# A fused two-layer gated block on one core: 16 bit integer outputs in the quantized feed-forward, the last norm in two parts with writes by ScalarE, and four banks for output products

## What is computed

```
x = x + tanh(g_xattn[0]) * attention0(layernorm(x), ctx)
x = x + tanh(g_ffn[0])   * experts(layernorm(x))          # 8 experts, top 2 of the first 1024 tokens
x = x + tanh(g_xattn[1]) * attention1(layernorm(x), ctx)
x = x + tanh(g_ffn[1])   * quantized_ffn(layernorm(x))
```

```
act_qdq(x)  : s = max(|x| over all of x) / 32767;  clip(round(x / s), -32768, 32767) * s
x    = act_qdq(x)
up   = act_qdq(x @ lpbq_dequant(w_up).T)          # w in 4 bits by blocks of 32
gate = act_qdq(x @ lpbq_dequant(w_gate).T)        # 768 wide
sig  = clip(round(sigmoid(gate) * 65536), 0, 65535) / 65536
gate = act_qdq(gate * sig)
o    = act_qdq(gate * up)
return o @ lpbq_dequant(w_down).T
```

## Time and profile before

| | us |
|---|---|
| median of 3 runs (lowest, highest) | 1007.83 (1006.88, 1008.12) |
| profiled execution, its own time | 1006.71 |
| its span, from first to last instruction | 1005.0 |
| PE busy | 882.8 (88%) |
| DVE busy | 667.8 (66%) |
| ACT busy | 476.6 (47%) |
| POOL busy | 215.9 (21%) |

### The profile page before, as it was taken

One profiled execution on the slowest core, in us unless ns is written; L12 is line 12 of the kernel. 1 busy time (PEld: TensorE's weight loads), 2 busy tenths in 40 slices (PEclk: granted clock), 3 DMA queues, 4 the chain that ended last, 5 costly groups with the idle time before them and its releaser, 6 DMA issues.

```text
span 1005.0 us, 13604 instructions
## 1 busy us (share of the span) xinstructions
PE 882.8 (88%) x4064; PEld 436.5 (43%) x4065; DVE 667.8 (66%) x1277; ACT 476.6 (47%) x613; POOL 215.9 (21%) x307
## 2 busy tenths in 40 slices
PE   4989999999984999999987789999999879992088
PEld 2542333333452666676754323333333454441077
DVE  5988888888451222222179798888887687697942
ACT  1232777777741121211221227777777554595750
POOL 3330111111128000000037212100004800185300
PEclk9895999999997999999998859999999999996589
DMA  7494745664435111111068773333330000000001
GB/s 227 138 279 73 201 117 161 172 168 135 127 110 167 32 32 31 31 31 31 26 215 219 187 184 76 76 76 76 75 75 2 1 1 0 1 0 0 0 32 53
DMA packets 71260, 91.45 MB, mean 91 GB/s; under 512 B 25894, under 2 KB 56870, under 8 KB 71206
## 3 DMA queue, kind: packets, MB, share of 16 engines
q1 hardware_dynamic: 62844, 67.38, 26.8%
q0 software_dynamic: 5584, 19.93, 6.0%
q10 hardware_dynamic: 2784, 3.54, 1.1%
HBM read 62.99 MB, written 27.44 MB: 90 GB/s over the span
## 4 chain that ended last, share of the span: by engine, by line
PE 72%; DVE 16%; ACT 4%; issue 3%; DMA 3%; POOL 2%; SPq 0%; DVEq 0%; ACTq 0%; POOLq 0%
PE PS L1383 12%; PE PS L1415 12%; PE PS L1404 11%; PE PS L1566 8%; PE PS L1544 8%; PE PS L1657 4%; PE PS L1640 3%; PE PS L1358 3%; PE PS L1502 2%; DVE MX L1026 2%; PE PS L1555 2%; DMA X<-in_x 2%; DVE stats L963 2%; PE PS L1429 1%; DVE Pt L1273 1%
## 5 line engine op out<-in xcount | busy, mean ns | idle before, releaser
L1026 DVE TENSOR_REDUCE MX<-PS 128x1 f32<-128x512 f32 x512 | 319.8, 683 | 42.5 <-PE PS L1383 41.1
L760 ACT ACTIVATE Pt<-PS 128x1024 f32<-128x1024 f32 x256 | 248.5, 1021 | 112.5 <-PE PS L1404 112.5
L1383 PE MATMUL PS<-KSt,BIG 96*128 96x512 bf16 x512 | 188.4, 414 | 9.3 <-DVE PS L1049 5.3
L1404 PE MATMUL PS<-BIG,KSt 99*128 99x512 bf16 x512 | 152.8, 385 | 1.1 <-DMA BIG<-MR 1.1
L1415 PE MATMUL PS<-Pt,VS 128*17 128x512 f32 x1024 | 136.1, 598 | 0.0
L1383 PEld LDWEIGHTS PS<-KSt,BIG 96*128 96x128 bf16 x512 | 41.0, 99 | 163.7 <-DVE MX L1026 108.1
L1121 DVE COPY Pt<-PS 128x512 f32<-128x512 f32 x46 | 29.7, 686 | 86.6 <-PE PS L1555 86.6
L1640 PE MATMUL PS<-KSt,BIG 128*128 128x512 f32 x192 | 83.2, 593 | 2.9 <-DVE KSt L1216 2.2
L1566 PE MATMUL PS<-BIG,Pt 128*128 x368 | 84.3, 382 | 1.1 <-DVE Pt L1121 1.0
L1544 PE MATMUL PS<-BIG,KSt 128*128 x184 | 84.1, 600 | 0.7 <-DVE KSt L1126 0.4
L597 POOL TENSOR_TENSOR MP<-MX,zrow 128x16 bf16<-128x16 f32 x32 | 7.0, 218 | 320.5 <-DVE MX L1026 320.5
(11 more groups left out here) (171 smaller groups left out, 1037.1 us busy)
## 6 DMA issues: line engine op xcount, KB each, us to landing
qk_parts<-BIG SPq DMA_DIRECT2D x64, 192.0 KB
BIG<-in_w POOLq DMA_DIRECT2D x12, 1024.0 KB, 5.9
BIG<-qk_parts SPq DMA_DIRECT2D x32, 192.0 KB, 3.4
KSt<-qk_parts SPq DMA_DIRECT2D x32, 192.0 KB, 3.8
v_rows<-BIG SPq DMA_DIRECT2D x8, 544.0 KB
VS<-v_rows SPq DMA_DIRECT2D x32, 136.0 KB, 2.9
BIG<-qk_parts SPq DMA_DIRECT2D x32, 128.0 KB, 3.9
KSt<-qk_parts SPq DMA_DIRECT2D x32, 128.0 KB, 3.9
```

Source lines behind the costliest of these rows:

```text
L760: act.activation(PP[:, 2 * (kc % 2) + half, :, :].rearrange("p h t -> p (h t)"), ST[half], ACT.Exp, scale=DK ** -0.5).then_inc(exp_done, 1)
L1026: dve.tensor_reduce(MX[:, g % 2, i % TB, i // TB:i // TB + 1], ring(i), AX.X, ALU.max, negate=True).then_inc(max_taken, 1)
L1383: pe.matmul(ring(i), QS[0:ROWS, g, h, qc * P:(qc + 1) * P], KS[0:ROWS, g, h, :], start=True, stop=True).then_inc(max_done, 1)
L1404: last = pe.matmul(ST[half][:, i * S:(i + 1) * S], KS[0:ROWS + PARTS, g, h, kc * P:(kc + 1) * P], QS[0:ROWS + PARTS, g, h, :], start=True, ...
```

## The change

- *Integer outputs.* ScalarE writes its scaled gate and up pieces straight into int16 buffers (`whole`, a ring of 4 pieces; `ups`, a ring of 8, where `xt` lay), VectorE writes the scaled sigmoid into uint16 (`steps`, a ring of 3). The conversion rounds and clips. `MAGIC`, its bias column and GpSimd's 38 passes go; VectorE's products read the integer pieces. `xt` and `o` are rounded as before.
- *Norm.* Two parts, tiles 0 to 9 and 10 to 15. VectorE makes `shift` = -mean x rstd, and ScalarE writes tiles 0 to 9 and 13 to 15 of `XF` as `X * rstd + shift`; VectorE writes 10 to 12. Statistics are spread between the updates.
- *Banks.* `tail` of both layers uses banks 2 to 5 in turn, and `project_out` waits for the update four tiles earlier.
- *Weights.* The first is transposed within the tail, the second after the joint maximum; the third's scales are taken just before the gate maxima, and it is transposed six banks later.
- *Order.* One up piece leads instead of three (`UP_EARLY`), and a product follows its own rounding pass instead of the next one's.

```diff
-FFN_A, FFN_B, FFN_C = range(0, 6), range(6, 12), range(12, NT)
+FFN_A, FFN_B = range(0, 10), range(10, NT)
+ACT_B = range(13, NT)
-UP_EARLY = 3
+W0_AT = 2 * TB + 2
+W2_AT = BANKS * 3 // 4
+UP_EARLY = 1
...
 # GpSimd
-for i in range(PIECES + 2):
-    if i <= PIECES:
-        gp.wait_ge(gate_magic, i + 1)
-        gp.tensor_scalar(ap, ap, -MAGIC, 1.0, ALU.add, ALU.mult).then_inc(gate_int, 1)
-    if i > 0:
-        gp.wait_ge(sig_round, i)
-        gp.tensor_scalar(sg, sg, -SIG_MAGIC, 1.0, ALU.add, ALU.mult).then_inc(sig_even, 1)
-for i in range(PIECES):
-    gp.wait_ge(up_magic, i + 1)
-    gp.tensor_scalar(ap, ap, -MAGIC, 1.0, ALU.add, ALU.mult).then_inc(up_int, 1)
...
 # ScalarE: end of attention, tail, norm
-if layer:
-    norm("ffn_a")
 copy_out(NG * B * (layer + 1) - 1, 1)
 for i in range(EARLY, NT):
     copy_turned(layer, i, i % 2)
-    if layer and i == NT - 2:
-        norm("ffn_b")
+    if layer and W0_AT <= i < W0_AT + 3:
+        copy_weight(0, i - W0_AT, 6 + (i - W0_AT) % 2)
+    if layer and i == FFN_A[-1] + 3:
+        norm("ffn_a")
...
+act.wait_ge(ln_rstd, 1)
+write_norm(FFN_A)
+norm("ffn_b")
+copy_nx(0)
+copy_nx(1)
+act.wait_ge(ln_rstd, 2)
+write_norm(ACT_B)
+copy_nx(2)
+copy_nx(3)
...
 # ScalarE: pieces
-act.activation(ap, ap, ACT.Identity, scale=sc[:, F_G:F_G + 1], bias=magic[:, 0:1]).then_inc(gate_magic, 1)
+wait(act, prod_done, i - SIGS + 1)
+act.activation(whole_piece(i), gate_piece(i), ACT.Copy, scale=sc[:, F_G:F_G + 1]).then_inc(gate_int, 1)
...
-act.activation(sig_piece(i - 1), gate_piece(i - 1), ACT.Sigmoid,
+act.activation(sig_piece(i - 1), whole_piece(i - 1), ACT.Sigmoid,
...
 # VectorE
-dve.tensor_scalar(sig_piece(i), sig_piece(i), SIG_MAX, SIG_MAGIC, ALU.min, ALU.add).then_inc(sig_round, 1)
+dve.tensor_scalar(steps_piece(i), sig_piece(i), SIG_STEPS, None, ALU.mult).then_inc(sig_round, 1)
 if 0 < i < PIECES:
     pair_max(i - 1)
-if i > 0:
-    product(i - 1)
+product(i)
...
-dve.scalar_tensor_tensor(ap, ap, MAGIC, piece(Q["up"], i), ALU.subtract, ALU.mult).then_inc(prod_done, 1)
+dve.tensor_tensor(ap, whole_piece(i + SIGS), ups_piece(i), ALU.mult).then_inc(prod_done, 1)
...
 # TensorE, tail
-elif i >= EARLY + 2:
-    pe.wait_ge(x_upd, t - 1)
+elif i == EARLY + 3:
+    pe.wait_ge(x_upd, NT * layer + EARLY)
+elif i >= EARLY + 4:
+    pe.wait_ge(x_upd, t - 3)
...
-project_out(layer, i - 1, 2 + (i - 1) % 2)
+project_out(layer, i - 1, 2 + (i - 1) % 4)
+if layer and W0_AT <= i < W0_AT + 3:
+    turn_weight(0, i - W0_AT, 6 + (i - W0_AT) % 2)
```

More of the change, by code:

```diff
@@ L828, in _, with write_norm, copy_nx @@
             tail(1)
[L831 to L840, removed]
+            def write_norm(some):
+                for i in some:
+                    t = x_tile(1, i)
+                    act.activation(XF[:, t, :], X[:, t, :], ACT.Identity, scale=rstd[:, i:i + 1],
+                                   bias=shift[:, i:i + 1]).then_inc(xf_act, 1)
+            def copy_nx(p):
                 b = ORDER[1][p]
@@ L893, in _ @@
             for i in range(PIECES):
-                ap = piece(Q["gate"], i)
-                act.activation(ap, ap, ACT.Identity, scale=sc[:, F_2:F_2 + 1], bias=magic[:, 0:1]).then_inc(gate_scaled, 1)
+                wait(act, prod_done, PIECES + 1 + i - SIGS + 1 if i >= SIGS else 0)
+                act.activation(whole_piece(i + SIGS), piece(Q["gate"], i), ACT.Copy,
+                               scale=sc[:, F_2:F_2 + 1]).then_inc(gate_scaled, 1)
                 scale_up(range(UP_EARLY + i, min(UP_EARLY + i + 1, PIECES)))
@@ L964, in norm_stats, with late_stats @@
                 return last
+            def late_stats(some):
+                for i in some:
+                    last = dve.bn_stats(stats[:, i, :], X[:, x_tile(1, i), :])
+                return last
             def norm(name, left=None):
@@ L987, in norm_rstd @@
-                link(dve, dve.reciprocal(rstd[:, :], nw2[:, :]))
-            def norm_write(tiles, to):
-                for i in tiles:
-                    dve.tensor_scalar(to[:, i, :], X[:, i, :], mv[:, i, 0:1], rstd[:, i:i + 1],
-                                      ALU.subtract, ALU.mult).then_inc(xn_ready, 1)
+                link(dve, dve.reciprocal(nw1[:, cols], sd[:, cols]))
+                link(dve, dve.tensor_tensor(nw2[:, cols], ve[:, cols], nw1[:, cols], ALU.mult))
+                link(dve, dve.tensor_tensor(nw1[:, cols], nw2[:, cols], sd[:, cols], ALU.add))
@@ L1477, in attention, with turn_weight @@
                 project_out(layer, EARLY - 1, 5)
+            def turn_weight(k, a, to):
+                if a == 0:
+                    pe.wait_ge(qw_ready, k + 1)
+                if k == 0:
+                    pe.wait_ge(o_ready, 2 * NG * B)
+                    wait(pe, qwt_ready, a - 1)
+                else:
+                    pe.wait_ge(x_upd, 2 * NT)
+                    pe.wait_ge(qwt_ready, 3 * k)
+                chunks = QC if k < 2 else KC
+                w = Q["raw"][:, k * QC * D:(k + 1) * QC * D].rearrange("p (c n) -> p c n", c=chunks)
+                for n in range(4 * a, 4 * a + 4):
+                    ci, co = n // chunks, n % chunks
+                    last = pe.transpose(bank(to)[:, n % 4 * P:(n % 4 + 1) * P],
+                                        w[:, co, ci * P:(ci + 1) * P], identf[:, :])
+                last.then_inc(qwt_turned, 1)
             def turn_tile(layer, i, to):
```

197 lines of the change are left out of this document (110 added, 87 removed).

## The result

| | before | after |
|---|---|---|
| median, us (4 runs each, same chip; lowest to highest) | 1007.43 (1006.88 to 1008.12) | 996.25 (995.76 to 997.09) |
| span of the profiled execution | 1005.0 | 994.1 |
| TensorE's mean granted clock | 0.925 | 0.931 |

The ratio is 0.9888, with a 95% interval of 0.9873 to 0.9902: 11.2 us faster, where the prediction said 12.4 and a total of 995.4. (The four runs of before are the three of "Time and profile before" and one more; hence 1007.43 and not 1007.83.)

The account below looks back on a forecast made before the run. The prediction took ScalarE to bound A's end, TensorE C, and VectorE's products D after the second product. Gains of 4.5 (A), 5.3 (C) and 2.6 (D), 12.4 us in all, off 1007.83 gave 995.4 us; range 991.5 to 1000.5.

Parts of the forecast that it names:

- C: Sigmoid beside the up products, 869 to 921.3 us: GpSimd's passes go, TensorE becomes the bound; 5.3 us gained.
- D: Gate times up, 921.3 to 957 us: one up pass leads, so the second product starts earlier; 2.6 us gained.
- A: The last norm, 791 to 822 us: new order, four banks and ScalarE's writes gain 4.5 us, bounds nothing and 6.
- The copy right behind its values: Start of the last norm: the last attention output's copy follows its values directly, starting at 792.5 us instead of 795.46.
- With four banks TensorE no longer waits for VectorE: Last norm: products 8 to 11, with three groups of weight transposes, end at 800.5 us without waiting for VectorE's updates.
- ScalarE bounds A from tile 15's copy on: End of the last norm: ScalarE's writes, root and copies take 8.7 us, until 814.1 us; joined maxima at 816.0.
- the 0.6 us of margin: Last norm: tile 15's copy taken to start at 805.0 us, not 804.4, as part may fall at the lower clock.
- B: The gate products, up to 869 us: nothing lost, though the third weight's scales and GpSimd's passes on it move there.
- the norm gives nothing: Rival, chance 0.12: ScalarE bounds the last norm, so only C and D gain; 999.9 us in total.
- slow rounding: Rival in C: rounding stays at 1.44 us without GpSimd, total 999.7; chance 0.08 shared with products of 1.52 us.
- double-rate products: Rival in D, chance 0.05: products on two 16 bit inputs run twice as fast; 2.4 us more gain, 993.0.
- slow integer writes: Rival in C and D, chance 0.03: integer writes slow ScalarE's passes; 1012.2 us at 0.7 us more per pass.

Follow-up runs that it names:

- own_updates: The changed kernel, with products 11 and 15 of the last norm waiting only for the update that used their bank; 993.80 us.
- two_banks: The changed kernel with two banks instead of four for output products in the last layer; 994.98 us.
- load_early: own_updates plus a one-column square root on ScalarE ahead of the copy of the last attention output, loading the table there; 992.42 us.
- both_late: The kernel before, with the last attention output's copy ahead of the square root and the third weight's scales moved behind the norm; 1004.71 us.
- int_only: The kernel before with only the integer outputs, their product order and the lead of one up piece, keeping the old last norm; 1001.82 us.
- root_three: load_early with the root of the first ten tiles moved ahead of the third weight copy; 991.64 us.

## Why the prediction was right, and where it was not

The total lies 0.9 us beside the forecast, inside the range. In C and D that is the forecast's mechanism and its size. In A the size nearly fits by luck, since the mechanism was another. Point by point:

- *The copy right behind its values*: right, 1.12 us.
- *"With four banks TensorE no longer waits for VectorE"*: this step failed. The waits decide, not the number of banks, and I had not run tiles 11 and 15 through the condition on bank 5, which the diff leaves standing. own_updates and two_banks show 2.32 and 1.63 us for it.
- *ScalarE bounds A from tile 15's copy on*: failed in the changed kernel. Tile 15's copy did start when forecast (13.37 us behind the values' start, for 13.57), with some luck: the 0.6 us of margin made room for the unforeseen 0.69 before product 11, and in own_updates the copy starts 12.45 behind. ScalarE's own path was sized well (ten writes 5.01 for 5.1, four copies 2.04 for 1.9, three writes 1.58 for 1.5), but "VectorE's own path is ready near 813, just ahead" was late: its writes came at 813.55, and behind them stand not one maximum of 1.74 but three, 2.93: the sum left out the two maxima of 512 columns. The stretch that was to stay under 12 us took 817.49 - 805.34 = 12.15.
- *4.5 us for A*: mis-sized in both directions. 3.75 came; 6.07 (29.27 less 23.20) would have with the wait mended, just over my bound of 6. Left out of the sum was what GpSimd's move gives: I had asked of it only whether B loses, though the prediction itself saw a VectorE pass slow down beside GpSimd in C. Two errors of opposite sign made the sum look better than its parts.
- *TensorE's idle stretches in A under 1.2 us*: not so. They are 1.23 before product 13, 1.52 before product 15 and 3.53 before the last transposes of the norm (814.38), which wait for VectorE's writes.
- *The table load*: right, 1.28 us at 802.11 and the root at 803.40, no drain. The 1380 ns of drain that the Trainium skill states (ScalarE: Activation LUTs, "What ACT_TABLE_LOAD costs") would, by the prediction's estimate, have made 996.8, closer to the total than my own, but not by this route: the trace after and load_early both contradict it.
- *B nothing*: right for the edit.
- *C 5.3, TensorE the bound*: right, 5.33. ScalarE's integer pass goes at the 1.04 taken (893.18 to 894.22), rounding takes 0.69 and the product 1.21. The mark "maxima joined 2.4 us before the first up pass" was put wrong: 2.44 is the last product's start (910.62); the join is 1.18 before, as in the kernel before.
- *D 2.6*: right, 2.64, and by the mechanism named.
- *The rivals*: "the norm gives nothing", slow rounding, double-rate products (1.23 each, no faster) and slow integer writes (1.13 to 1.15) are all excluded by the rows.
- *Not in the sum at all*: attention's end comes 0.54 later and B takes 0.27 more. The other kernels show that such shifts come without an edit.

## What to carry to other kernels

When banks or buffers are renumbered, evaluate every condition that names one for every index: a wait that is too strong stays correct and silently takes back the gain. Before costing an engine at "hidden", look in the trace for tiny instructions that take far longer than their equals; here two ends that coincide, VectorE's and GpSimd's, named the culprit, and taking the other engine's work away may be worth more than reordering. And compare kernels between marks around the edit, since such stretches repeated here within hundredths where the totals move by a microsecond or two.

## What the hardware did that I had not expected

**VectorE held behind GpSimd.** Instructions of 10 or 16 columns took 0.73, 1.56, 2.64 and 1.02 us instead of 0.17, each ending 0.03 us behind a GpSimd pass over SBUF. Reciprocals, statistics and updates that read PSUM beside such passes kept their lengths. The Trainium skill (SBUF — State Buffer, "Who interferes with whom") states this: a VectorE instruction with two SBUF inputs contends with a GpSimd instruction that reads SBUF, and so does a `tensor_scalar` in a 2-port mode; whichever came first keeps the shared ports to its end, and the other stands still. The traces agree, down to the 0.17 us without GpSimd in both_late; in which mode the `tensor_scalar` passes ran they don't show.

**The clock in untouched code.** Three kernels, the same stretch of 596 to 604 us (the columns are those of the earlier trace rows): before, after, int_only.

```profile
596.00:604.00 8.00, 7.09 (x31) 2.32 (x30) 5.38 (x10) 4.44 (x5) 3.62 (x8) 0.68 0.10 35
```

```profile
596.00:604.00 8.00, 7.47 (x26) 2.50 (x26) 4.62 (x8) 4.61 (x5) 3.62 (x8) 0.55 0.02 6
```

```profile
596.00:604.00 8.00, 7.01 (x17) 2.08 (x17) 5.65 (x10) 2.72 (x3) 3.60 (x8) 0.50 0.32 113
```

The granted clock in it is 0.68, 0.55 and 0.50 (0.50 is the 1.2 GHz level), although the diff leaves this code alone. TensorE is back at full clock at 601.1 us in before, at 603.2 in the changed kernel and at 604.8 in int_only, and V follows at 791.43, 791.97 and 793.99. The clock is not all of it. int_only starts the products of the second attention 1.4 us later than before does (578.42 against 576.99), though no edit touches what lies ahead, and the remaining 1.1 of its 2.6 us come between there and V. In the changed kernel they start 1.0 earlier (575.95), and 1.6 are lost behind it. Why the starts differ stays open.

The other shifts go with the clock too. B took 49.98 us in the three traces with a granted clock of 1.00 over it and 50.25 to 50.69 in the eleven with 0.95 to 0.99. The end took 50.05 at 0.93 and 51.39 to 51.61 in the five traces at 0.90. This is not a property of one kernel: 17 executions of before alone, on one chip beside root_three, ran from 1005.98 us (clock 0.925) to 1014.00 (0.919). Whether each kernel also tends to its own value is not settled, with one profile each.
